# Three gathers a head cover part of their tokens, and SyncE fetches the other 81 rows

## The reference

```
scores, idx = top_k(sim, 16)                       # for both halves of the key
final_scores, pk_idx = top_k(score, 16)            # over the 16 x 16 sums
k = einsum('bnhk,bnhkd->bnhd', softmax(final_scores), keys_table[ind])
v = einsum('bnhk,bnhkd->bnhd', softmax(final_scores), values_table[ind])
sim = einsum('bihd,bjhd->bhij', q, k)              # causal mask, softmax
out = einsum('bhij,bjhd->bhid', softmax(sim), v)   # then @ Wo, added to x
```

## Time and profile before

| what | value |
|---|---|
| median of 2 runs | 10075.28 us (10074.95 to 10075.61) |
| span of the profiled execution, from its first instruction to its last | 10059.9 us |
| the execution's own time beside its span | only the two runs' times are given; their median is 15.4 us above the span |
| POOL busy | 7544.0 us, 75% |
| DVE busy | 6956.2 us, 69% |
| PE busy (matmul) | 5726.9 us, 57% |
| ACT busy | 3087.9 us, 31% |
| mean granted TensorE clock | 0.748 of full speed |

### The profile page before, as it was taken

The page is one execution under the profiler, slowest core; times in us unless marked ns, Lnnn a source line. Parts: engine busy times, 40 slices in busy tenths (PEclk is TensorE's granted clock), DMA queues, the critical chain, the costliest instruction groups (busy, mean ns, idle before and its releaser), DMA issues.

```text
span 10059.9 us, 190416 instructions
## 1 busy us (share of the span) xinstructions
PE 5726.9 (57%) x23108; PEld 4551.2 (45%) x23108; DVE 6956.2 (69%) x42844; ACT 3087.9 (31%) x9770; POOL 7544.0 (75%) x7957
## 2 busy tenths in 40 slices
PE   5655555555555555555555555555555555555555
PEld 4544444444444444444444444444444444444444
DVE  8876667666666677676776666767667676666664
ACT  4333233233333333333333333333333332322222
POOL 5777777777777777777777777777777777777776
PEclk7877777777777777777777777777777777777777
DMA  3333343333433334333343333333333333333333
GB/s 109 105 109 109 109 114 109 109 109 109 113 109 109 109 109 113 109 109 109 109 113 109 109 109 109 113 109 109 109 111 111 110 109 109 109 111 109 109 109 100
DMA packets 503669, 1100.92 MB, mean 109 GB/s; under 512 B 196992, under 2 KB 246912, under 8 KB 502144
## 3 DMA queue, kind: packets, MB, share of 16 engines
q0 software_dynamic: 381120, 1041.22, 36.4%
q1 hardware_dynamic: 71488, 31.70, 1.3%
q10 hardware_dynamic: 49664, 16.42, 0.8%
HBM read 1084.36 MB, written 4.19 MB: 108 GB/s over the span
## 4 chain that ended last, share of the span: by engine, by line
POOL 73%; issue 24%; DVE 1%; PE 1%; POOLq 0%; DMA 0%; ACT 0%; ACTq 0%; SPq 0%; DVEq 0%
POOL ring L353 73%; DVE hot L1013 0%; DMA wo<-in_Wo 0%; POOLq L369 0%; PE ps_o L724 0%; ACTq L492 0%; POOLq L367 0%; DVE ps_v L935 0%; DMA ring<-in_table,idx 0%; PE ps_p L610 0%; PE ps_p L614 0%; DVE nmax L1064 0%; PE ps_s L748 0%; POOLq L368 0%; DVE cand L987 0%
## 5 line engine op out<-in xcount | busy, mean ns | idle before, releaser
L353 POOL DMA_INDIRECT ring<-in_table,idx x7940 | 7542.5, 950 | 2491.2 <-issue 2420.6
L671 PE MATMUL ps_w<-ring,diag 128*128 128x256 f32 x8192 | 2151.7, 423 | 13.0 <-issue 8.7
L715 PE MATMUL ps_p<-ident,prob 128*128 128x128 f32 x2304 | 564.7, 400 | 2304.0 <-ACT prob L453 2296.3
L671 PEld LDWEIGHTS ps_w<-ring,diag 128*128 128x128 f32 x8192 | 1740.6, 218 | 297.1 <-issue 19.7
L1013 DVE SCALAR_TENSOR_TENSOR hot<-rank,posf,cand 128x54 f32<-128x54 f32 x8192 | 1654.5, 271 | 0.3
L715 PEld LDWEIGHTS ps_p<-ident,prob 128*128 128x128 f32 x2304 | 395.1, 202 | 2501.0 <-ACT prob L453 1600.2
L932 DVE TENSOR_SCALAR ps_v<-ring,wgt 128x256 f32<-128x256 f32 x512 | 248.4, 485 | 1837.0 <-DMA ring<-in_table,idx 1836.8
L935 DVE SCALAR_TENSOR_TENSOR ps_v<-ring,wgt,ps_v 128x256 f32<-128x256 f32 x3072 | 1478.9, 481 | 19.6
L444 ACT ACTIVATE diag<-ident,wgt 128x128 f32<-128x128 f32 x4096 | 1251.8, 391 | 0.0
L453 ACT ACTIVATE prob<-ps_s,nmax 128x128 f32<-128x128 f32 (+7 forms) x512 | 378.1, 738 | 2300.8 <-issue 2259.6
L724 PEld LDWEIGHTS ps_o<-probT,kv 128*128 128x128 f32 x4608 | 986.7, 304 | 144.9 <-ACT probT L461 81.6
(11 more groups left out here) (119 smaller groups left out, 8141.2 us busy)
## 6 DMA issues: line engine op xcount, KB each, us to landing
far<-in_table SPq DMA_DIRECT2D x16352, 1.0 KB
far<-in_table ACTq DMA_DIRECT2D x15904, 1.0 KB
ring<-in_table,idx POOLq DMA_INDIRECT x7940
xin<-in_x SPq DMA_DIRECT2D x8, 512.0 KB
mask<-in_adj SPq DMA_DIRECT2D x1, 4096.0 KB, 15.9
out_x<-acc SPq DMA_DIRECT2D x64, 64.0 KB
far_row<-far_at SPq DMA_DIRECT2D x128, 0.5 KB
far_row<-far_at ACTq DMA_DIRECT2D x124, 0.5 KB
```

What stands on the lines that cost most here:

```text
L353: pool.indirect_dma_start(out=ring[:, t % RING, k, :], out_offset=None, in_=table, in_offset=bass.IndirectOffsetOnAxis(ap=idx[:, t, k:k + ...
L671: ins = nc.tensor.matmul(pw_ps, diag[:, k, :], ring[:, t % RING, k, :], start=(k == 0), stop=(k == PE_ROWS - 1))
L715: ins = nc.tensor.transpose(ps_p[:, c, (j % 4) * P:(j % 4 + 1) * P], prob[:, j * P:(j + 1) * P], ident[:])
```

## The change

The 16th row of units 1, 2 and 6 is no longer gathered for all 128 tokens. From head 1 on, POOL's 16th gather of these units covers the first 127, 112 and 64 tokens, and its place is `far` and no longer the ring's slot. SP fetches the last 1, 16 and 64 rows by single transfers, as it does for units 3 and 7. The number of gathers stays as it is. SP's sets now come in the order of units 1, 2, 3, 6 and 7 (SP_ORDER holds set numbers: 4, 5, 0, 6, 1), and in head 1 in the order of units 0, 1, 2, 3, 4, 6 and 7. DVE waits for so many single rows as were not gathered.

```
+PARTS = (1, 2, 6)
+PART_ROWS = (127, 112, 64)
+SETS = FAR + NEAR + PARTS
+GATHERED = (0,) * len(FAR + NEAR) + PART_ROWS
+SP_ORDER = (4, 5, 0, 6, 1)
+SP_FIRST_ORDER = (2, 4, 5, 0, 3, 6, 1)
...
-                for q in range(0, stop, LOADED):
+                start = GATHERED[i]
+                for q in range(start // 4 * 4, stop, LOADED):
+                    rows = min(LOADED, stop - q)
...
-                    for j in range(LOADED):
+                    for j in range(max(start - q, 0), rows):
                         sp.dma_start(far[q + j:q + j + 1, i, :].bitcast(U8), table_bytes[bass.ds(at[j], KV_BYTES)]) \
                             .then_inc(far_dma[i], 16)
...
+            def far_sets(n, order, follows):
+                for j, i in enumerate(order):
+                    if j + 1 < len(order):
+                        far_begin(n, order[j + 1])
+                    elif follows is not None:
+                        far_begin(n + 1, follows)
+                    far_fetch(n, i, P - LOADED if SETS[i] == NEAR[1] else P)
 
             def turn(b):
-                far_sets((b + 1) * HEADS, range(0, last_set))
+                n = (b + 1) * HEADS
+                far_sets(n, SP_ORDER[:2], None)
+                far_begin(n, SP_ORDER[2])
+                far_sets(n, SP_ORDER[2:4], None)
+                far_begin(n, SP_ORDER[4])
                 stores(b)
-                far_sets((b + 1) * HEADS, range(last_set, last_set + 1))
+                far_begin(n + 1, SP_ORDER[0])
+                far_fetch(n, SP_ORDER[4])
 
             load(1)
-            far_begin(1, last_set + 1)
-            far_fetch(1, last_set + 1)
-            far_begin(1, 0)
-            far_begin(1, last_set + 2)
-            far_fetch(1, 0)
-            far_begin(1, 1)
-            far_fetch(1, last_set + 2, P - LOADED)
-            far_begin(2, 0)
-            far_fetch(1, 1)
+            far_begin(1, SP_FIRST_ORDER[0])
+            far_sets(1, SP_FIRST_ORDER, SP_ORDER[0])
...
-                for k in range(TOPK if first or t not in SETS else FAR_ROW):
+                for k in range(TOPK if first or t not in FAR + NEAR else FAR_ROW):
+                    rows, place = P, ring[:, t % RING, k, :]
+                    if t in PARTS and k == FAR_ROW and not first:
+                        rows = GATHERED[SETS.index(t)]
+                        place = far[0:rows, SETS.index(t), :]
                     pool.indirect_dma_start(
-                        out=ring[:, t % RING, k, :], out_offset=None, in_=table,
-                        in_offset=bass.IndirectOffsetOnAxis(ap=idx[:, t, k:k + 1], axis=0)) \
+                        out=place, out_offset=None, in_=table,
+                        in_offset=bass.IndirectOffsetOnAxis(ap=idx[0:rows, t, k:k + 1], axis=0)) \
                         .then_inc(pe_rows_dma[t] if k < PE_ROWS else dve_rows_dma[t], 16)
...
-                    dve.wait_ge(far_dma[SETS.index(t)], P * 16)
+                    dve.wait_ge(far_dma[SETS.index(t)], (P - GATHERED[SETS.index(t)]) * 16)
                     dve.sem_clear(far_dma[SETS.index(t)])
```

More of the change, by code:

```diff
@@ L34 @@
 NEAR = (0, 4)
-SETS = FAR + NEAR
+PARTS = (1, 2, 6)
[4 more added lines that the diff above has]
+SP_FIRST_ORDER = (2, 4, 5, 0, 3, 6, 1)
 NEAR_UNITS = 4
@@ L220, in gathered @@
         def gathered(n, t):
-            return n * (TOPK - PE_ROWS - (t in SETS)) * 16 + (TOPK - PE_ROWS) * 16
+            return n * (TOPK - PE_ROWS - (t in FAR + NEAR)) * 16 + (TOPK - PE_ROWS) * 16
         HALVES = [1 + (t >= 4) for t in range(TILES)]
@@ L287, in far_fetch @@
                     sp.sem_inc(sp_mark, 1)
-                for q in range(0, stop, LOADED):
+                start = GATHERED[i]
+                for q in range(start // 4 * 4, stop, LOADED):
+                    rows = min(LOADED, stop - q)
                     _, at = nc.values_load_multi_w_load_instructions(
-                        far_row[0:1, i, q:q + LOADED], engines=[mybir.EngineType.SP],
+                        far_row[0:1, i, q:q + rows], engines=[mybir.EngineType.SP],
                         min_val=0, max_val=(HEADS * NUM_KV - 1) * KV_BYTES,
@@ L321, in _ @@
-            far_fetch(1, 1)
+            far_begin(1, SP_FIRST_ORDER[0])
+            far_sets(1, SP_FIRST_ORDER, SP_ORDER[0])
             with sp.Fori(2, HEADS) as h:
-                far_sets(h, range(len(FAR)))
+                far_sets(h, SP_ORDER, SP_ORDER[0])
             with sp.Fori(0, BATCH - 2) as b:
@@ L327, in _ @@
                 with sp.Fori(1, HEADS) as h:
-                    far_sets((b + 1) * HEADS + h, range(len(FAR)))
+                    far_sets((b + 1) * HEADS + h, SP_ORDER, SP_ORDER[0])
             turn(BATCH - 2)
             with sp.Fori(1, HEADS - 1) as h:
-                far_sets((BATCH - 1) * HEADS + h, range(len(FAR)))
-            far_sets(BATCH * HEADS - 1, range(len(FAR)), True)
+                far_sets((BATCH - 1) * HEADS + h, SP_ORDER, SP_ORDER[0])
+            far_sets(BATCH * HEADS - 1, SP_ORDER, None)
             stores(BATCH - 1)
```

## The result

The changed kernel takes 10182.03 us (2 runs, 10181.87 to 10182.18) against 10075.28 us: ratio 1.0107, 95% interval 1.0088 to 1.0126. It is slower by 1.1%, inside the stated range and short of 2%. The forecast of 10080 us missed by 102 us. The times are only 106.8 us apart, because the two timed runs before stand 15.4 us above the profiled span and those of the changed kernel 2.0 us above theirs. In the 32 runs of the kernel before that went with the experiments, on two chips, it took 10055 to 10064 us, and once 10084; what made its first two runs longer isn't known.

The account below looks back on a forecast made before the run. POOL's gathers and the issue gaps between them were taken to bound the kernel; 10075 - 15 (64-row gathers) + 20 (start) = 10080 us, with an 8 in 10 range of 10035 to 10190 us.

Parts of the forecast that it names:

- rival B: POOL's 16th gather of unit 1: 127 rows on one engine's ring cost +1.3 to +5.0 us a head; chance 0.21.
- The forecast's own bracket: Whole kernel: forecast together with partial gathers costing as much as whole ones, 10060 to 10110 us; chance 0.56.
- The bound: POOL's gathers and the issue gaps between them make 97% of the path that sets the end.
- The price of the partial gathers: POOL's three cut gathers: 0 saved for 127 and 112 rows, 0.24 us a head for 64 rows, 15 us in all.
- the base: Whole kernel: span 10059.9 us, with the runs' median 15.4 us above it, carried over unchanged.
- The 64 rows: POOL's gather of 64 rows in unit 6: 0.24 us saved a head, 15 us in all.
- Its second half: Unit 1's gather of 127 rows: POOL also waits until one engine drains its 7.4 us, 466 us, 10546.
- The start: SP late in head 1: POOL loses 10.4 and 9.4 us at units 3 and 4 of head 2, 20 us together.
- The sign that I had named: POOL's waits for L946, the sum line, grow from 12.6 to about 33 us, all before 500 us.
- SP's load and order: SP in a steady head: 337 rows and five begins take 142 us of 155.6, hidden behind POOL's gathers.
- The landing of the 127 rows: Rows of unit 1's cut gather land up to 7 us later, well inside POOL's lead: cost 0.

Follow-up runs that it names:

- experiment 5: The kernel before, 16th gathers of units 1, 2, 5 and 6 cut to 126, 125, 124 and 120 rows, nobody fetching the rest: 10128.16 us.
- experiment 6: The kernel before, 16th gathers of units 1, 2, 5 and 6 cut to 113, 96, 16 and 8 rows, nobody fetching the rest: 10132.8 us.
- experiment 3: The changed kernel with whole gathers into the ring; SP still fetches the 1, 16 and 64 rows, DVE waits but sums the ring's slot: 10074.38 us, ratio 1.0015.
- experiment 8: experiment 3 with SP issuing unit 0's rows in head 1 before it waits for unit 1's indices: 10061.96 us, ratio 1.0002.
- experiment 1: The kernel before, 16th gathers of units 1, 2 and 6 cut to 127, 112 and 64 rows, nobody fetching the rest: 10151.38 us, ratio 1.0091.

## Why the prediction was right and where it failed

- **The range and the forecast.** 10182.03 us lies in the range of 10035 to 10190, because the range took in the lower half of rival B. The forecast's own bracket, 10060 to 10110 at 0.56, doesn't hold it.
- **The bound.** Right. POOL's chain set the end before and after, and its time is the sum of its gathers with their gaps, so 1.6 us more in one gather of 124 showed in full.
- **The price of the partial gathers.** This is the step that failed: "The gathers of 127 and 112 rows are nearest to the row of 128, so I take 0 for them." For 112 rows it was right (0.93 us, 0.02 less). For 127 rows it cost 1.61 us a head, 102 us in all. "Nearest" was measured in rows, while the price goes by the rows of the fullest engine, where 112 is 7, 128 is 8 and 127 is 127.
- **The miss of 102 us.** That it equals this one term is luck, since four smaller misses cancel: 11 us less saved at the 112 and 64 rows (4 in place of 15) and 14 us in the whole gathers, which no term had, against 11 us less lost near the start (8.8 in place of 20) and 13 us of the base. The prediction carried 15.4 us over from the span to the time, and the changed kernel had 2.0.
- **The 64 rows.** Sized at 0.24 us saved and measured at 0.04: 3 us in place of 15. Nearly all of a gather's 0.95 us is paid once: 16 rows still cost 0.85.
- **Rival B.** It was this one, at 0.21: its place, its size of +1.3 to +5.0 us a head, of which the lower end came (+1.6), and its mechanism with one correction. Not every count that 16 doesn't divide goes to one engine: by experiments 5 and 6, 126, 125, 124 and 120 rows behave as if 14, 5, 4 and 15 engines shared them. Its second half, that POOL waits for one engine to drain, didn't happen: the gap behind the long gather is 0.30 us like all others. The rule that the Trainium skill states (DMA: Bandwidth & Descriptors, section "Why a DMA increments its semaphore by 16 and not by 1") agrees with experiments 5 and 6: with the engines that it gives, 14, 5, 4, 15, 1, 16, 16 and 8, all eight durations come out to 0.04 us. Its exception for some direct copies doesn't show in these gathers. What the Trainium skill says in its section "Anatomy of one DMA — SWDGE (gpsimd) path" on the same page, that many descriptors can be had before their cost shows, held for 8 steps against 1 (0.1 us) and not for 127.
- **The start.** 20 us foretold, 12.4 measured, in the two units that were named (3 and 4 of head 2), as 5.0 + 7.4 against 10.4 + 9.4. Unit 7's sum ended at 450.8 and not 459.5. I had counted a begin of 3.0 us before unit 0's rows, whose addresses were long there (begun at 204.7), and 3.0 for each later one, where those of the short fetches take 1.4 and 2.1; a set of 64 takes 23.1 and not 24.2; landing takes about 1 us and not 3.1. The sign that I had named, POOL's waits for the sum line growing to 33 us, didn't come: the profile puts the two new waits under "issue". Experiments 3 and 8 show the cause.
- **SP's load and order.** Right: 142 us foretold, 139 measured, no wait of POOL's in the steady part. At a turn in mid-kernel the stores are issued by 5199.0 us and DVE overwrites the accumulator at 5235.5, without waiting.
- **The landing of the 127 rows.** Cost 0, as foretold: POOL waits for no sum in a steady head.

## What to carry to other kernels

Where the time is one engine's instruction count times a nearly fixed step, making an instruction smaller is worth next to nothing and leaving one out is worth most of its step: 123 gathers in place of 124 gave 0.5% once the helpers kept up, three smaller ones lost 1.1%. Keep the partitions of a gather a multiple of 16, or at least a number with a large divisor up to 16: 120 and 126 rows cost 0.04 us more than 128, but 113 cost 1.4 and 127 cost 1.6. Before more work goes to a helper's queue, add up its loop in full, turns and begins too, and count the first round by itself, when it isn't yet ahead: a stall there was never given back to POOL, which never rests afterwards.

## What the runs showed of the hardware

A gather cost POOL 0.84 us + 0.0136 us for each row of its fullest engine (worked out from 128, 112 and 127 rows, tested on eight other sizes, to 0.04 us), and a prime 113 rows took 2.36 us where 96 took 0.92. Which engines moved the rows no trace shows; their number is inferred from these times and from the packet counts below.

The other engines aren't idle meanwhile. The packets of experiment 1, with those of less than 512 B:

```profile
DMA packets 532901, 1096.18 MB, mean 108 GB/s; under 512 B 227232, under 2 KB 277152, under 8 KB 531376
```

Before, 196992 were under 512 B. The difference is 30240 = 63 x 480, and 480 is 15 x 32. This fits one engine that gets its 127 rows in 32 packets while each of the other 15 gets 32 packets too, which are tiny. Packets of 4 rows and one to complete on each of 16 engines give 64, 128, 144 and 48 for 126, 125, 124 and 120 rows, where the whole gather has 48; that makes 192 more a head, and 381120 + 63 x 192 = 393216 is the count of experiment 5. For 113, 96, 16 and 8 rows the same rule gives 480, 48, 32 and 32, 400 more a head, and 381120 + 63 x 400 = 406320 is the count of experiment 6. That POOL writes one step of all 16 lists at once, with fillers where a list has nothing, fits both the counts and the durations; it was inferred, not seen. A price by packets in place of rows fits nearly as well (to 0.05 us over the twelve sizes), and only the small gathers speak against it as the whole story: 64 and 16 rows have the same number of packets and took 0.90 and 0.85 us.
